# Output copies behind the transposed probabilities, and a third output tile, in a cross-attention stage on one core

## What is computed

```python
x = x + window_attention(layernorm(x))          # 16 heads of 32, 2 key groups, windows of 64
x = x + cross_attention(layernorm(x), ctx)      # the part that the change touches
x = x + top1_expert(layernorm(x))               # 8 experts of 512 x 512, gate = the largest softmax
# cross_attention: 8 key heads of 128, each shared by 2 query heads
q = (h @ Wq).reshape(32, 112, 16, 128);  k = (ctx @ Wk).reshape(32, 375, 8, 128);  v = (ctx @ Wv) likewise
attn = softmax(where(mask, q @ k.T / sqrt(128), -inf));  out = (attn @ v).reshape(32, 112, 2048) @ Wo
```

## Time and profile before

| | us |
|---|---|
| median of 3 runs (2687.05 to 2689.24) | 2688.05 |
| the profiled execution | 2685.35 |
| its span | 2683.7 |
| PE busy | 2482.7 (93%) |
| PEld busy | 2257.6 (84%) |
| DVE busy | 1733.0 (65%) |
| ACT busy | 1241.2 (46%) |
| POOL busy | 1030.1 (38%) |

### The profile page before, as it was taken

The page is one execution under the profiler, slowest core; times in us unless marked ns, Lnnn a source line. Parts: engine busy times, 40 slices in busy tenths (PEclk is TensorE's granted clock), DMA queues, the critical chain, the costliest instruction groups (busy, mean ns, idle before and its releaser), DMA issues. The chain is left out here.

```text
span 2683.7 us, 46237 instructions
## 1 busy us (share of the span) xinstructions
PE 2482.7 (93%) x14850; PEld 2257.6 (84%) x14851; DVE 1733.0 (65%) x4899; ACT 1241.2 (46%) x3183; POOL 1030.1 (38%) x1424
## 2 busy tenths in 40 slices
PE   6899897799999999999999999999999999979488
PEld 5888886788989898889989898898989888869376
DVE  7878886565575657566575756656565665644466
ACT  4555553454454545445454545445454454522211
POOL 4334443243343434334353534334343343431422
PEclk9999998899999999999999999999999999975699
DMA  8322332412122112212121211111111111122654
GB/s 256 95 71 84 96 108 89 162 50 66 62 75 66 62 54 74 74 52 83 52 91 58 88 55 53 54 41 55 51 57 54 53 55 41 41 72 70 220 178 129
DMA packets 108892, 217.87 MB, mean 81 GB/s; under 512 B 20336, under 2 KB 48720, under 8 KB 108416
## 3 DMA queue, kind: packets, MB, share of 16 engines
q1 hardware_dynamic: 103440, 188.42, 21.9%
q0 software_dynamic: 5040, 16.58, 1.7%
q10 hardware_dynamic: 224, 10.49, 1.2%
HBM read 134.57 MB, written 91.36 MB: 84 GB/s over the span
## 5 line engine op out<-in xcount | busy, mean ns | idle before, releaser
L1171 POOL TENSOR_SCALAR x_probs<-x_probs,x_inv 112x376 f32<-112x376 f32 x512 | 639.3, 1258 | 273.6 <-DVE x_inv L1323 273.6
L1165 POOL TENSOR_SCALAR x_bias<-x_top 112x1 f32<-112x1 f32 x512 | 129.1, 252 | 871.8 <-DVE x_top L1295 864.9
L1215 ACT ACTIVATE x_probs<-x_probs,x_bias 112x376 f32<-112x376 f32 x512 | 307.0, 603 | 105.2 <-POOL x_bias L1165 104.7
L1380 PE MATMUL x_ps_o<-x_pT,x_v 128*128 128x224 f32 (+1 forms) x2304 | 310.3, 279 | 43.2 <-DVE x_pT L1302 42.5
L1380 PEld LDWEIGHTS x_ps_o<-x_pT,x_v 128*128 128x128 f32 (+1 forms) x2304 | 288.0, 192 | 69.6 <-DVE x_pT L1302 61.5
L1380 PE MATMUL x_ps_f<-x_xT,x_wq 128*128 128x448 f32 x1536 | 339.3, 371 | 4.5 <-issue 4.5
L1380 PE MATMUL x_ps_f<-x_wo,x_oT 128*128 128x512 f32 x1344 | 315.7, 391 | 1.0 <-DVE x_oT L1311 1.0
L1380 PE MATMUL x_ps_s<-x_kT,x_qT 128*112 128x376 f32 x1536 | 314.6, 340 | 1.5 <-DVE x_top L1295 1.5
L1380 PE MATMUL x_ps_f<-x_ctxT,x_wk 128*128 128x376 f32 x1536 | 306.4, 335 | 1.9 <-DVE x_ctxT L1272 1.9
L1380 PEld LDWEIGHTS x_ps_f<-x_xT,x_wq 128*128 128x128 f32 x1536 | 282.4, 189 | 26.5 <-issue 4.7
L1380 PEld LDWEIGHTS x_ps_f<-x_wo,x_oT 128*128 128x128 f32 x1344 | 252.6, 189 | 50.0 <-issue 1.2
(11 more groups left out here) (186 smaller groups left out, 3799.5 us busy)
## 6 DMA issues: line engine op xcount, KB each, us to landing
x_ctxs<-x_ctxT SPq DMA_DIRECT2D x32, 752.0 KB, 3.8
x_ctxT<-x_ctxs SPq DMA_DIRECT2D x32, 752.0 KB, 4.3
x_xT<-h2T SPq DMA_DIRECT2D x16, 896.0 KB, 5.0
m_rows<-slots SPq DMA_DIRECT2D x35, 258.0 KB, 3.0
slots<-w_blank SPq DMA_DIRECT2D x8, 1032.0 KB, 5.2
x_ctxn<-in_ctx_dram SPq DMA_DIRECT2D x32, 256.0 KB
m_hn<-in_L_ffn_W_dram SPq DMA_DIRECT2D x32, 256.0 KB
w_xa<-in_x_dram SPq DMA_DIRECT2D x32, 224.0 KB, 3.3
```

What stands on the lines that cost most here:

```text
L1165: pool.tensor_scalar(bias[:, m:m + 1], top[:, m:m + 1], -0.1 * NEG, -SCALE, ALU.max, ALU.mult) \
L1171: pool.tensor_scalar(probs[0:T, m, 0:SE], probs[0:T, m, 0:SE], inv[:, m:m + 1], None, ALU.mult).then_inc(normed, 1)
L1215: act.activation(probs[0:T, m, 0:SE], probs[0:T, m, 0:SE], ACT.Exp, bias=bias[:, m:m + 1], scale=SCALE, accum_out=total[:, m:m + 1]).then_ ...
L1380: last = pe.matmul(out, w, r, start=m == 0, stop=m == len(jobs) - 1)
```

## The change

- `RING` is three output tiles instead of two.
- O goes from g = 2 to g = 3, C from g = 3 to g = 2.
- On ScalarE the exponentials come first in a step, on VectorE the inverses directly behind the maxima; both ahead of the early fills.
- `probsT(i - 1)` stands ahead of `out(i - 2)` on both.
- Pieces of x (`x_piece`) go to g = 1 and 2 of batches with b % 4 = 1 and 2, instead of all four steps of b % 4 = 1, and stand at the end of the step, as do the splits of weights. The mask row of a batch is made at the end of step 1 of the batch before it.
- `wk` holds one half. Its pieces are by head pair (128 columns, all rows) instead of by 128 rows, four instead of two; those of half 1 are loaded in batch 30, each when its K fill of batch 31 is done, and split at the end of the steps (30,1) to (31,0).

```diff
--- before.py
+++ after.py
@@ -882,10 +882,10 @@
     NB = HALVES * B
     STEPS = NB * G
     TILES = B * T // P
-    RING = 2 * P
+    RING = 3 * P
     SCALE = float(1.0 / np.sqrt(D))
     mdt = mask.dtype
-    assert B * T % RING == 0 and B % QUAD == 0 and SE > S and T * 2 <= RING
+    assert B * T % P == 0 and B % QUAD == 0 and SE > S and T * 3 <= RING
 
     def last_batch(tile):
 
@@ -898,9 +898,9 @@
     def early_fills(i):
         b, g = divmod(i, G)
         out = [("K", b + 1, g)] if b + 1 < NB else []
-        if g == 3 and b + 2 < B:
+        if g == 2 and b + 2 < B:
             out += [("C", b + 2, 0), ("C", b + 2, 1)]
-        if g == 2 and b in TILE_OF:
+        if g == 3 and b in TILE_OF:
             out.append(("O", TILE_OF[b], 0))
         return out
 
@@ -939,15 +939,15 @@
         n = min(T, RING - at)
         return [(0, n, at)] + ([(n, T, 0)] if n < T else [])
 
-    PIECES = {"k": CC, "v": CC, "q": KC, "o": H // 2}
-    FIRST_SPLITS = [("k", 0, n) for n in range(CC)], [("q", 0, n) for n in range(KC)], [("v", 0, n) for n in range(CC)]
+    PIECES = {"k": G, "v": CC, "q": KC, "o": H // 2}
+    FIRST_SPLITS = [("k", 0, n) for n in range(G)], [("q", 0, n) for n in range(KC)], [("v", 0, n) for n in range(CC)]
 
     def splits_at(i):
         b, g = divmod(i, G)
         if b == 0:
             return [("o", 0, g)]
-        if b == B - 8 and g < CC:
-            return [("k", 1, g)]
+        if 0 <= i - G * (B - 2) - 1 < G:
+            return [("k", 1, i - G * (B - 2) - 1)]
         if b == B - 3:
             return [("q", 1, g)]
         if i == G * B:
@@ -967,7 +967,9 @@
     def x_piece(i):
 
         b, g = divmod(i, G)
-        return b // QUAD + 1 if b % QUAD == 1 and b // QUAD + 1 < NB // QUAD else None
+        if b // QUAD + 1 == NB // QUAD or b % QUAD not in (1, 2) or g not in (1, 2):
+            return None
+        return b // QUAD + 1, 2 * (b % QUAD - 1) + g - 1
 
     ctxs = nc.dram_tensor("x_ctxs", [B, P, 2 * CC * SE], F32, kind="Internal").ap()
 
...
-        wk = sb("wk", [P, HALVES, 2, CC, G * D], F32R)
+        wk = sb("wk", [P, 2, CC, G * D], F32R)
         wv = sb("wv", [P, 2, CC, G * D], F32R)
         wq = sb("wq", [P, 2, KC, H * D], F32R)
         wo = sb("wo", [P, 2, H, C], F32R)
@@ -1026,13 +1028,15 @@
         def weight(piece):
 
             kind, half, n = piece
-            return [{"k": lambda: wk[:, half, a, n, :], "v": lambda: wv[:, a, n, :], "q": lambda: wq[:, a, n, :],
+            return [{"k": lambda: wk[:, a, :, n * D:(n + 1) * D], "v": lambda: wv[:, a, n, :], "q": lambda: wq[:, a, n, :],
                      "o": lambda: wo[:, a, 2 * n:2 * n + 2, :]}[kind]() for a in (HI, LO)]
 
         def weight_source(piece):
             kind, half, n = piece
-            if kind in "kv":
-                return (Wk if kind == "k" else Wv)[n * P:(n + 1) * P, half * G * D:(half + 1) * G * D]
+            if kind == "k":
+                return Wk[:, (half * G + n) * D:(half * G + n + 1) * D].rearrange("(c p) d -> p c d", p=P)
+            if kind == "v":
+                return Wv[n * P:(n + 1) * P, half * G * D:(half + 1) * G * D]
             if kind == "q":
                 return Wq[n * P:(n + 1) * P, half * H * D:(half + 1) * H * D]
             rows = half * H * D + 2 * n * D
...
-                    if b == B - 12:
-                        for n in range(PIECES["k"]):
-                            load_w(("k", 1, n))
                     if b == B - 4:
                         sp.wait_ge(fill_ready, until(("Q", B // QUAD - 1, H - 1)))
                         for n in range(PIECES["q"]):
@@ -1144,6 +1145,10 @@
                         load_ctxT(b + 2)
                     if b + 2 < NB:
                         load_mask(b + 2)
+                    if b == B - 2:
+                        for n in range(PIECES["k"]):
+                            sp.wait_ge(fill_ready, until(("K", B - 1, n)))
+                            load_w(("k", 1, n))
                     if b in TILE_OF:
                         store(TILE_OF[b])
                     if b == B:
@@ -1230,22 +1235,22 @@
                 for p in FIRST_SPLITS[2]:
                     split(p)
                 for i in range(STEPS):
-                    for p in splits_at(i):
-                        split(p)
+                    exps(i)
                     for f in early_fills(i):
                         if f[0] != "O":
                             fill(f)
-                    exps(i)
-                    if x_piece(i) is not None:
-                        split_x(x_piece(i), i % G)
-                    if i >= 2:
-                        out(i - 2)
                     for f in before_transposes(i):
                         fill(f)
                     if i >= 1:
                         probsT(i - 1)
+                    if i >= 2:
+                        out(i - 2)
                     for f in behind_transposes(i):
                         fill(f)
+                    if x_piece(i) is not None:
+                        split_x(*x_piece(i))
+                    for p in splits_at(i):
+                        split(p)
                 out(STEPS - 2)
                 probsT(STEPS - 1)
                 out(STEPS - 1)
@@ -1336,29 +1341,30 @@
                     fill(f)
                 for p in FIRST_SPLITS[2]:
                     split(p)
+                mask_row(0)
                 for i in range(STEPS):
-                    if i % G == 0:
-                        mask_row(i // G)
                     maxima(i)
-                    for p in splits_at(i):
-                        split(p)
+                    inverses(i)
                     for f in early_fills(i):
                         if f[0] != "O":
                             fill(f)
-                    inverses(i)
-                    if x_piece(i) is not None:
-                        split_x(x_piece(i), i % G)
                     for f in early_fills(i):
                         if f[0] == "O":
                             add(f)
-                    if i >= 2:
-                        out(i - 2)
                     for f in before_transposes(i):
                         fill(f)
                     if i >= 1:
                         probsT(i - 1)
+                    if i >= 2:
+                        out(i - 2)
                     for f in behind_transposes(i):
                         fill(f)
+                    if i % G == 1 and i // G + 1 < NB:
+                        mask_row(i // G + 1)
+                    if x_piece(i) is not None:
+                        split_x(*x_piece(i))
+                    for p in splits_at(i):
+                        split(p)
                 out(STEPS - 2)
                 probsT(STEPS - 1)
                 out(STEPS - 1)
@@ -1369,8 +1375,8 @@
                 pe.wait_ge(ident_done, 2)
                 seen = [0]
 
-                def weights(kind, half):
-                    n = split_all(kind, half)
+                def weights(kind, half, piece=None):
+                    n = split_all(kind, half) if piece is None else SPLIT_NO[kind, half, piece] + 1
                     if seen[0] < n:
                         pe.wait_ge(w_lo, n)
                         seen[0] = n
@@ -1393,13 +1399,13 @@
                                                 ident[0:rows, 0:rows])
                     elif kind == "K":
                         half = at // B
+                        weights("k", half, n)
                         if n == 0:
-                            weights("k", half)
                             if half:
                                 pe.wait_ge(ctxT_in[at % 2], 16 * ((at - B) // 2 + 1))
                             else:
                                 pe.wait_ge(fill_done, until(("C", at, 1)))
-                        last = product(out[:, 0:SE], [(wk[:, half, a, c, n * D:(n + 1) * D], ctxT[:, at % 2, b_, c, :])
+                        last = product(out[:, 0:SE], [(wk[:, a, c, n * D:(n + 1) * D], ctxT[:, at % 2, b_, c, :])
                                                       for c in range(CC) for a, b_ in PASSES])
                     elif kind == "V":
                         weights("v", at // B)
@@ -1415,7 +1421,7 @@
                     else:
                         weights("o", at // TILES)
                         pe.wait_ge(o_lo, G * (last_batch(at) + 1))
-                        slot = at % 2 * P
+                        slot = at * P % RING
                         last = product(out[:], [(oT[:, a, h, slot:slot + P], wo[:, b_, h, :])
                                                 for h in range(H) for a, b_ in PASSES])
                     last.then_inc(fill_ready, 1)
```

## The result

The changed kernel takes 2695.32 us (median of 8 runs, 2692.62 to 2696.73), the kernel before 2687.55 us (8 runs of the same comparison, 2684.76 to 2689.24). The ratio is 1.0028, 95% interval 1.0018 to 1.0039: slower, by 7.8 us, where 13.4 were forecast. The profiled execution took 2695.32 us with a span of 2693.5, so 10.0 more than the one of before.

A forecast was written before the change was run, and what follows sets the result against it. TensorE bounds the stage, so only its waits can change. Steady quads +2.8, quad 0 +6.2, quads 28 and 32 +2.3 each: +13.6 on 2685.35 us, 2698.9; plus 2.7 for the median, 2701.5, range 2683 to 2714.

The forecast's parts named there:

- K copies behind the inverses: VectorE's light step, K copy moved behind the inverses: cycle 4.33 us, 0.6 longer, against TensorE's 3.57.
- Q fills: Half 0, b % 4 = 3, g=2: Q fill waits 1.39 us for K's bank, 1.45 with restart, 7 quads.
- K(b,3): K fill for head pair 3, half 0: waits 0.44 us for g=2's K copy, 0.49 with restart, twice a quad.
- Products of (b,1): P·V product of head pair 1, after a light step: 0.35 us late, some 0.46 with restart, twice a quad.
- rival 2: Order of pT and out does count, or bank waits are half: about -13 us, 2688, no change; chance 0.2.
- Batches without O: Batches 1, 9, 17 and so on: late products lose 3.06 us in half 0, 3.3 in half 1, with restarts.
- Swap of pT and out: pT ahead of out on VectorE: the product is released by the end of out, so the swap alone is worth 0.
- M = S + 1.66: Light step after an O step: VectorE's first maximum starts 1.66 us after the scores start, against 1.34 before.
- The alternation of C, O and light steps: Rival: interleaving unlike steps makes all 13 steady quads gain 1.9 us, time 2663; chance 0.03.
- The wk load: Batch 30: piece 0 issued about 1 us into (30,2), takes about 4.7; scores of (30,3) some 3.1 us late.
- rival 3: TensorE's clock falls after each wait of 1.4 us and more: +24 us, 2725; chance 0.09 for more than +12.
- Quad 60, head, and behind: Head and tail: two more k loads and split pairs about +0.7 us, last batch -0.7, together 0.

The follow-up runs named there:

- both order edits undone: Changed kernel with K and C copies again ahead of exponentials and inverses, and out(i-2) again ahead of probsT(i-1): 2653.69 us, ratio 0.9886.
- mask rows back: Changed kernel with both order edits undone and each batch's mask row made again at its first step, ahead of the maxima: 2642.41 us, ratio 0.9891.

## Why the prediction was right

The forecast was slower by 13.4 us, at 2701.5; it was slower by 7.8, at 2695.3, within the range and past the 0.2%. (The forecast's own terms give 2701.65, 0.15 more than its last figure.) Its quads against the profiles, in us of change:

| | forecast | measured |
|---|---|---|
| quad 0 | +6.2 | +5.8 |
| half 0, with O (4, 12, 20) | +0.8 | 0.0 |
| half 0, one batch without (8, 16, 24) | +7.4 | +5.6 |
| quad 28 | +2.3 | +3.0 |
| quad 32 | +2.3 | +1.3 |
| half 1, with O (36, 44, 52) | -5.7 | -5.7 |
| half 1, one without (40, 48, 56) | +0.6 | -0.6 |
| quad 60 and the tail | -1.0 | -3.3 |
| ahead of the first scores | +0.7 | +1.5 |
| behind the stage | 0 | +2.3 |
| sum | +13.6 | +9.9 |

The direction and the causes are as forecast, but part of the closeness is luck. In the quads the forecast had +12.9 and the profiles have +6.1; outside them it had +0.7 and they have +3.8, which no term explains, and the two misses offset each other in part.

**K copies behind the inverses.** Right in mechanism, the step that carries the sign. VectorE's cycle is 4.19 and not 4.33: the K copy starts at M + 2.60 where 2.7 was taken, and the output columns keep VectorE from its next instruction for 0.30, not 0.37. That 0.14 is the common cause of the sizes that were off: the maxima of a step that came too late were late by 0.1 less with each light step.

**Q fills.** By starts 1.34 late, step 1.45 longer, seven times; forecast 1.39 and 1.45. (The bracket's 1.17 is shorter only because it counts from the product's modelled end.) The maxima start 1.84 behind the scores, as forecast, and the run with those seven K copies early takes 10.0 us off.

**K(b,3).** 9.44 against 9.10, 0.34 lost, forecast 0.49 (ready at 5.84, wanted at 5.40). In quads 4, 12 and 20 this term and the next come twice and are 0.6 us less than forecast. That is the +0.8 that didn't come, and more: 0.06 in each light step behind an O step (3.63 for 3.57) and 0.07 to 0.14 at the (b,1) of b % 4 = 0, which the forecast had at nothing, take some of it back. In quads 8, 16 and 24, which were 1.8 short together, they make 0.3 a quad, and the late steps below the rest.

**Products of (b,1).** 0.28 late and 0.29 lost, forecast 0.35 and 0.46: the restart cost almost nothing on so short a wait, where I had added 0.1 as after a long one. Over the whole execution `x_oT` ends 38 of the products' waits and `x_pT` one, as forecast; rival 2, that out does not hold the product, falls with it.

**Batches without O.** In half 0 the three late steps (9,3), (10,0) and (10,1) take 5.07, 4.73 and 8.44 us against 3.57, 3.57 and 7.94 clean: 3.16 lost, where 0.49 for K(b,3) and 3.06 were forecast. That is 0.4 less a quad, of the same 0.14 a cycle. In half 1 it turned the +0.6 to -0.6.

**Swap of pT and out.** This step failed as it was written. "The swap alone is worth 0" holds for the release of the product, which waits for both. It doesn't hold for the step: alone, the swap costs 9.4 us on the kernel before and 8.9 on the changed one. What it costs is VectorE's idle time before the transposes, in which `out` used to run; the maxima come 0.29 later. The prediction had this effect (M = S + 1.66, measured 1.60) but booked it under the new order of O and C, and so took the swap for harmless. The sum was not hurt; the advice to a reader would have been.

**The alternation of C, O and light steps.** I gave this 0.03 as a rival, with a time of 2663, and alone it gives 2664.8: -21 us, the largest gain in the change. The forecast contained it only net of what the K copies cost in the same steps, and half 1, where no C fills stand between the K copy and the fill that reuses its bank, shows it (-5.7, as forecast). Moving the x splits brought some 8 us more. So the change is +9 for the swap and +34 for the copies, against some -21 for the alternation (with the third tile and the halved `wk`, which were not taken apart from it) and -10 (0.9923 to 0.9886) for the x splits and what was moved with them. These make some +12; measured +8. The copies alone cost 42 on the kernel before and 34 undone on the changed one, so that the parts do not add up exactly.

**The wk load.** Issue at 1420.30, 1.03 behind the start of (30,2), forecast about 1; landed 4.2 later at most, forecast 4.7; step (30,2) 3.2 longer than without the wait (the bracket has 2.99), forecast 3.1. What was missed is the clock behind it, another 1.6 us. The clock was rival 3, and of the waits of over 1 us in quads 0 to 56 it followed this one alone; the fall of the earlier trace rows is gone with the wait of the earlier trace rows. So quad 28 swapped one fall for another, and the chance of 0.09 for a general fall was ample. (Rival 3 counts 6 waits at Q, of which there are 7; with 7 it has +26 instead of +24.) The Trainium skill, "TensorE: Matmul & The Clock Gate", HAM oscillation, has idle gaps put TensorE to half clock; the trace agrees in this place, and not after any of the seven Q waits.

The fall does not follow this wait every time. Seven of the kernels have it, of 2.86 to 3.07 us; in five of the profiles the clock fell behind it and (30,3) took 10.62 to 10.69 us, in two (both order edits undone, 2.88; mask rows back, 2.90) it stayed at 1.00 and (30,3) took 9.08 and 9.10.

**Quad 60, head, and behind.** Of the -3.3 of quad 60 only a part is the change. The kernel before had a second fall of the clock, which the forecast did not see (it counts one place). Its last step, in the table by stretches of before:

```profile
2382.00:2385.00 3.00, 1.92 (x10) 1.57 (x10) 1.41 (x3) 1.26 (x3) 0.00 (x0) 0.50 0.00 0
2385.00:2388.00 3.00, 2.09 (x9) 1.82 (x9) 0.39 (x1) 0.36 (x1) 0.00 (x0) 0.50 0.00 0
```

The step takes 19.72 us there, and 16.49 in the run of the swap alone, which has the same fills there and no fall; after the change it takes 22.42, and 20.87 in the run with the wk pieces loaded sooner. Without the falls, and if the swap moves the last step by little, quad 60 is some 110.4 us before and 108.8 after: -1.6, forecast -1.0. So both kernels have two falls in these steps, and by such differences they cost before some 4.9 us (1.7 of the forecast's estimate at (29,1), and 3.2) and after 3.1. The head's +1.5 and the +2.3 behind the stage are not terms of the change that I can show. The head's code differs by two loads and splits, but its first scores start anywhere from 510.2 to 513.8 in the profiles of kernels with the same head, and the time behind the stage goes from 287.3 to 290.6 in kernels with the same code there.

**What would have shown it wrong** was named as products released by pT, no waits at fills, no clean half 1, or a low clock in many places. None of them came.

## What to carry to other kernels

Where an engine's work stands in a fixed order, a wait in the middle of a chain across engines (maxima, bias, exponential, sum) is a place to put work into, up to the length of the wait. A copy of 0.55 us that stood there cost the chain nothing, and moved behind it delayed all that followed and each bank that it frees, for 34 to 42 us over 256 steps. Three copies of 1.4 us in the same place made the chain 0.67 longer, and still paid. Before swapping two copies, ask of each whether it runs in the engine's idle time, and not only which of them the next consumer waits for. Where a change has several parts, price each alone: here two good ones (steps of different kinds alternating, splits off the light step) hid behind two bad ones, and without these the kernel is 1.1% faster, and 1.8% with its loads and splits placed too.

## What the runs showed of the hardware that I had not expected

- A wait of TensorE of 2.99 us was followed by 4 us at a granted clock of 0.60 and 0.55, and cost 1.6 us more than the wait itself. The same wait at 2.88 and 2.90 us in two other kernels was followed by none. Nor was one of 1.81 at (33,1) in the kernel before, while one of 1.86 in the same place in the run of the swap alone was; its step takes 11.59 us for 9.99. The seven waits of 1.17, and one of 1.76 in quad 0, had none. So the length of the wait alone does not decide it.
- Two kernels with the same code and the same waits there ended the last step in 22.4 us in one execution and 20.9 in the other, by the clock alone (0.60 in 4 us of one, 1.00 in the other). In the kernel before a fall of the clock made it 3.2 longer than in the run of the swap alone. The end of a stage is worth no reading finer than that from one profile.
- Counted by starts, a late start of a product or fill cost its step little more than its own length: 0.28 us late cost 0.29, 1.29 late (the product of (5,1) before, bracket 1.14) cost 1.35, and 1.34 late (Q fills, bracket 1.17) cost 1.45. The bracket of the idle time is the shorter measure, since it counts from a modelled end.
